# Two of a step's four stores begun by ScalarE's queue instead of the sync engine's, in the node stage of a four-layer graph network

## The chip, the cores and the metric

The kernel runs on one core of one Trainium2 chip. A core has TensorE (PE in the profile), VectorE (DVE), ScalarE (ACT), GpSimd (POOL) and the sync engine (SP), each with an instruction stream of its own that runs in the order in which it was written, and 16 DMA engines that move data between HBM and the on-chip memory. The engines meet through semaphores. A DMA is begun ("issued") by an instruction on one of the streams; the data then moves beside whatever that stream does next. The metric is the time of one execution in microseconds on the device, as the median of several runs.

## The reference, cut to what matters

Four layers of a graph network update 100,000 nodes of 160 numbers (64 scalars and 32 vectors of three). There are 25,000 edges, sorted by their destination. Layers 0 to 2 all have this form:

```python
sc = concat(xs @ W_self0 * a / sqrt(64), einsum(xv, W_self1) * a / sqrt(32))   # every node
conv = ...                                       # sums over a node's incoming edges
x = layernorm(x + sc + alpha * conv)             # every node
```

Layer 3 normalizes each node, adds attention over the incoming edges, and ends with a feed-forward block:

```python
x = node_input + proj(attention over incoming edges)
s2, v2 = eq_layernorm(x)
fs, fv = linear(s2, v2)                          # times the node's attribute a
y = x + linear(silu(fs[:, :128]), fv * sigmoid(fs[:, 128:]))
x = layernorm(node_input + y)
```

A node without an incoming edge needs no edge term in any layer. So the kernel first takes every node through all four layers as if it had no edges (the node stage), and keeps the rows before layers 1, 2 and 3 as tables in HBM; later stages gather rows of these tables for the edges and write over the rows of destination nodes.

## The kernel before, in words

`program` runs its stages one after the other, with a barrier between them: weights, the node stage (`all_nodes`), the index of the edges, three edge layers, and four stages for the attention. The change is in `all_nodes` alone.

`all_nodes` works on 250 nodes at a time, 125 partitions by J = 2 rows. There are eight lanes (buffers for eight such groups), and 100,000 / 2,000 = 50 rounds, so 400 lane steps. What one lane step does, each as a small function of lane n and round i:

- SP: `load` (L574 to L582) begins three transfers: `nodes_s_t` (65 partitions by 250 numbers, from a transposed copy of x), `nodes_v_t` (97 partitions by 250) and `nodes_z` (125 partitions by 2 rows of 164 numbers, from `rows`). `store1`, `store2` and `store3` (all L588) write the 125 by 2 rows before layers 1, 2 and 3 to their tables; `store_out` (L592 to L595) writes 125 by 2 rows of 160 numbers from `nodes_res` to `out`. That is seven transfers per lane step.
- DVE: `sum0` (L663) waits for the three loads of its lane and sums the rows; `add0` to `add2` (L673) add a layer's product from PSUM to the row; `widen0` to `widen2` (L683, L685) finish the variance, after which the row may be stored; then parts of layer 3.
- ACT: `var0` to `var2` (L749) square the rows, `copy1` and `copy2` (L738, L739) bring the transposed rows back from PSUM, `scale`, `ffn_copy` and `activate` serve layer 3, and `finish` (L759) writes the result to `nodes_res`.
- PE: transposes and products (L795, L796, L812, L814, L312 to L338). POOL: the mean (L612), roots, and part of layer 3.

The order on every engine comes from one table, `order`: each function has a begin, in planned units, with a spacing of `part = 8.40` between lanes. `staggered` folds the begins of all lanes into one round of 8 x 8.40 and sorts them, and `run_rounds` gives each engine its own functions in that order, in a loop over rounds. A begin therefore sets only the place of a function among the others of its engine. On SP this gives in every lane step: `load` of one lane, then `store3`, `store_out`, `store2` and `store1` of lanes that were loaded earlier. A store waits for the engine that wrote its rows (`widen` on DVE, `finish` on ACT); `add` of the next round waits until the store from that buffer has landed (`stored`), and so does `finish` (`out_stored`). At the end of the stage SP waits for all stores.

Of the kernel before, what the change touches and what calls it, by code (L numbers as in the profile page):

```python
# [14 lines left out]
J = 2  # L15
# [23 lines left out]
def count_at(t, i, engine, step):  # L39

    names = t["names"][engine]
    return i * len(names) + names.index(step) + 1


def prime(eng, t, engine):

    for n in range(t["lanes"]):
        eng.sem_inc(t[engine][n], len(t["names"][engine]))


def gate(eng, t):


    eng.sem_inc(t["turn"], 1)


def staggered(order, part, lanes):

    steps = []
    for step, begin in order:
        for n in range(lanes):
            behind, at = divmod(begin + n * part, lanes * part)
            steps.append((at, int(behind), n, step))
    return [(step, n, behind) for at, behind, n, step in sorted(steps, key=lambda entry: entry[0])]


def run_rounds(eng, rounds, order, part, steps, lanes=LANES):  # L70

    mine = [(step, n, behind) for step, n, behind in staggered(order, part, lanes) if step in steps]
    for step, n, behind in mine:
        if not behind:
            steps[step](n, 0)
    with eng.Fori(1, rounds) as i:
        for step, n, behind in mine:
            steps[step](n, i - behind)  # L80
    for step, n, behind in mine:
        if behind:
            steps[step](n, rounds - 1)
# [412 lines left out]
def all_nodes(nc, sem, sb, banks, inp, w, ffn, tables, out, nodes):  # L496
# [3 lines left out]
    lanes = NODE_LANES  # L500
    rounds = nodes // NODE_ROWS
    T = lanes * J
    x_loaded = [sem(f"nodes_x_loaded_lane{n}") for n in range(lanes)]
    stored = {l: [sem(f"nodes_table{l}_stored_lane{n}") for n in range(lanes)] for l in (1, 2, 3)}
    out_stored = [sem(f"nodes_out_stored_lane{n}") for n in range(lanes)]
    ready = sem("nodes_constants_ready")

    part = 8.40
    order = [("load", 0.0), ("sum0", 10.65), ("mean0", 11.22), ("mult0", 13.01), ("add0", 14.19), ("var0", 15.04),
# [4 lines left out]
             ("double", 39.85), ("measure", 40.25), ("merge", 41.02), ("square", 41.63), ("widen", 41.96),  # L514
             ("roots", 42.28), ("root_attr", 43.53), ("scale", 43.8), ("normalize", 44.7), ("ffn_turn", 46.14),
             ("ffn_copy", 48.01), ("hidden", 50.4), ("activate", 52.9), ("gates", 55.33), ("ffn_out", 56.65),
             ("residual", 58.87), ("out_measure", 59.72), ("out_merge", 60.47), ("out_widen", 66.09),
             ("out_roots", 66.34), ("offset_out", 67.99), ("finish", 70.39), ("store_out", 71.47)]

    done = {"pe": {"ffn_turn": "ffn_turned", "hidden": "ffn_hidden", "ffn_out": "ffn_out"},  # L520
            "act": {"scale": "ffn_scaled", "ffn_copy": "ffn_copied", "activate": "ffn_activated",
# [8 lines left out]
    for l in range(3):  # L530
# [3 lines left out]
    t = lane_steps(sem, "nodes", lanes,  # L534
                   **{e: [done[e][step] for step, begin in order if step in done[e]] for e in done})
# [6 lines left out]
    z = sb("nodes_z", [P, 4, T, ROW])  # L542
# [6 lines left out]
    root3 = sb("nodes_root3", [P, T])  # L549
    factor3 = sb("nodes_factor3", [P, T])  # L550
    offset3 = sb("nodes_offset3", [P, T])
# [4 lines left out]
    res = sb("nodes_res", [P, T, F])  # L556
    out_view = out.rearrange("(p r) f -> p r f", p=P)
    table_view = [x.rearrange("(p r) f -> p r f", p=P) for x in tables]
    x_t = inp["x_t"]

    def tiles(n):
        return slice(J * n, J * n + J)

    with nc.Block() as block:
        @block.sync
        def _(sp):
            for n in range(lanes):
                for l in (1, 2, 3):
                    sp.sem_inc(stored[l][n], 16)
                sp.sem_inc(out_stored[n], 16)  # L570
            sp.wait_ge(ready, 2)

            def load_x(n, i):

                sp.wait_ge(t["dve"][n], count_at(t, i, "dve", "added0"))
                gate(sp, t)
                rows = bass.ds(i * T + J * n, J)
                sp.dma_start(s0_t[0:VS, n, :].rearrange("f (j p) -> f j p", j=J), x_t[0:VS, rows, :]
                             ).then_inc(x_loaded[n], 16)
                sp.dma_start(v0_t[0:V + 1, n, :].rearrange("f (j p) -> f j p", j=J), x_t[MEAN:X, rows, :]  # L580
                             ).then_inc(x_loaded[n], 16)
                sp.dma_start(z[:, 0, tiles(n), :], table_view[0][:, rows, :]).then_inc(x_loaded[n], 16)  # L582

            def store_table(l):
                def store(n, i):
                    sp.wait_ge(t["dve"][n], count_at(t, i + 1, "dve", f"widened{l - 1}"))
                    gate(sp, t)
                    sp.dma_start(table_view[l][:, bass.ds(i * T + J * n, J), :], z[:, l, tiles(n), :]  # L588
                                 ).then_inc(stored[l][n], 16)
                return store  # L590

            def store_out(n, i):  # L592
                sp.wait_ge(t["act"][n], count_at(t, i + 1, "act", "out_normed"))
                gate(sp, t)
                sp.dma_start(out_view[:, bass.ds(i * T + J * n, J), :], res[:, tiles(n), :]  # L595
                             ).then_inc(out_stored[n], 16)

            run_rounds(sp, rounds, order, part, dict(load=load_x, store_out=store_out, store1=store_table(1),
                                                     store2=store_table(2), store3=store_table(3)), lanes)
            for n in range(lanes):  # L600
                for l in (1, 2, 3):
                    sp.wait_ge(stored[l][n], 16 * rounds + 16)
                sp.wait_ge(out_stored[n], 16 * rounds + 16)
# [126 lines left out]
        @block.scalar  # L730
        def _(act):
            prime(act, t, "act")
            act.wait_ge(ready, 2)

            def copy(l):
                def copy_turned(n, i):
                    act.wait_ge(t["pe"][n], count_at(t, i + 1, "pe", f"turned{l}"))
                    act.activation(s_t[0:VS, n, :], banks[n % 2][0:S + 1, 0:W], ACT.Copy)  # L738
                    act.activation(v_t[0:V + 1, n, :], banks[n % 2][0:V + 1, W:2 * W], ACT.Copy  # L739
                                   ).then_inc(t["act"][n], 1)  # L740
                return copy_turned

            def square_rows(l):

                def step(n, i):
                    act.wait_ge(t["dve"][n], count_at(t, i + 1, "dve", f"added{l}"))
                    for j in range(J):
                        k = J * n + j
                        ins = act.activation(x3[:, k, :], z[:, l + 1, k, 0:X], ACT.Square,  # L749
                                             bias=z[:, l + 1, k, MEAN:MEAN + 1], scale=-1.0,  # L750
                                             accum_out=total[:, l, k:k + 1])
                    ins.then_inc(t["act"][n], 1)
                return step

            def finish(n, i):
                act.wait_ge(t["dve"][n], count_at(t, i + 1, "dve", "out_offset"))
                act.wait_ge(out_stored[n], 16 * i + 16)
                for j in range(J):
                    ins = act.activation(res[:, J * n + j, :], ffn["y"][:, n, j, :], ACT.Identity,  # L759
                                         bias=out_offset[:, n, j:j + 1], scale=ffn["y_root"][:, n, j:j + 1])  # L760
                ins.then_inc(t["act"][n], 1)

            def scale(n, i):
                ffn_scale(act, ffn, t, i + 1, n, [x3[:, J * n + j, VS:X] for j in range(J)],
                          z[:, 3, tiles(n), A:A + 1].rearrange("p j o -> p (j o)"))

            run_rounds(act, rounds, order, part, dict(
                copy1=copy(1), copy2=copy(2), var0=square_rows(0), var1=square_rows(1), var2=square_rows(2),
                scale=scale, finish=finish,
                ffn_copy=lambda n, i: ffn_copy_turned(act, ffn, t, i + 1, n),  # L770
                activate=lambda n, i: ffn_activate(act, ffn, t, i + 1, n)), lanes)
# [1866 lines left out]
```

## Time and profile before

| | us |
|---|---|
| Median of three runs (11,328.65 to 11,331.06) | 11,330.98 |
| Profiled execution, its own time | 11,326.82 |
| Span of that execution, first to last instruction | 11,325.1 |
| Node stage within the span, about 47 to 4,674 | 4,627 |
| All later stages, 4,674 to the end | 6,651 |

Over the whole span PE is busy for 80%, DVE for 72%, POOL for 47% and ACT for 40% of the time. The node stage makes up about two fifths of the span and is steady: windows of 1,000 us from 500 us to 4,500 us differ by less than 2% in every engine's busy time. In the tables below, the idle time of an engine is given with what ended it ("<-"), and a DMA issue on SP is shown as `SPq ... DMA_DIRECT2D`; the duration of an issue is the time that the issuing instruction took, not the time in which the data moved.

### The profile page before, as it was taken

How to read it: one execution, taken by the hardware profiler on the slowest of the kernel's cores; microseconds unless marked ns; L12 is line 12 of the kernel's file. 1: busy time of each engine (PE TensorE's matmuls, PEld its weight loads, DVE VectorE, ACT ScalarE, POOL GpSimd, SP SyncE). 2: the span in 40 equal slices, each digit the busy share in tenths (PEclk: the TensorE clock that was granted, in tenths of full speed). 3: DMA queues.
4: the chain of work that ended last, by engine and by line, in shares of the span. 5: the costliest groups of instructions: out<-in, count | busy, mean ns of one | idle time of the engine just before them, and what ended most of it. 6: DMA issues, size and time to landing. Idle time of an engine off the chain costs nothing. (4 is left out here: it accounts for less than half of the span.)

```text
span 11325.1 us, 241587 instructions
## 1 busy us (share of the span) xinstructions
PE 9089.1 (80%) x58771; PEld 8291.2 (73%) x58771; DVE 8098.2 (72%) x40535; ACT 4475.4 (40%) x17107; POOL 5279.8 (47%) x6680
## 2 busy tenths in 40 slices
PE   7877787777778787799978887888588888849998
PEld 6777777777777777688866676777577777738888
DVE  5666666666666666688878887888688888877777
ACT  4555555555555555333322232333222222212222
POOL 3444444444444444577755554555444444423444
PEclk8888888888888888899999998999888888869999
DMA  2222222222222222233322222222111111111111
GB/s 68 85 86 85 85 86 85 86 86 85 86 86 85 86 85 85 70 77 77 77 63 68 68 67 59 57 57 57 39 40 40 39 39 40 39 32 51 53 54 48
DMA packets 988491, 753.89 MB, mean 67 GB/s; under 512 B 430970, under 2 KB 948478, under 8 KB 988048
## 3 DMA queue, kind: packets, MB, share of 16 engines
q1 hardware_dynamic: 823696, 587.78, 18.4%
q0 software_dynamic: 164352, 162.20, 6.0%
q14 instruction: 409, 3.35, 0.1%
q8 instruction: 34, 0.56, 0.0%
HBM read 362.41 MB, written 392.80 MB: 67 GB/s over the span
## 5 line engine op out<-in xcount | busy, mean ns | idle before, releaser
L749 ACT ACTIVATE nodes_x<-nodes_z 125x161 f32<-125x161 f32 x2400 | 1005.5, 422 | 1439.1 <-DVE nodes_z L673 1437.4
L127 PE MATMUL bank<-ident 128*128 128x128 f32 x10000 | 1478.0, 297 | 97.1 <-PEq L883 58.7
L127 PEld LDWEIGHTS bank<-ident 128*128 128x128 f32 x10000 | 1415.1, 213 | 145.5 <-issue 59.2
L814 PE MATMUL bank<-self_v,nodes_v_t 128*125 128x98 f32 x4800 | 1153.2, 328 | 0.0
L812 PE MATMUL bank<-self_s,nodes_s_t 128*125 128x65 f32 x4800 | 977.2, 291 | 150.9 <-DVE ffn_y L233 143.6
L812 PEld LDWEIGHTS bank<-self_s,nodes_s_t 128*125 128x125 f32 x4800 | 879.8, 223 | 226.6 <-issue 206.4
L612 POOL TENSOR_SCALAR nodes_z<-nodes_sum 125x2 f32<-125x2 f32 x400 | 113.2, 283 | 1987.4 <-DVE nodes_sum L663 1987.4
L673 DVE SCALAR_TENSOR_TENSOR nodes_z<-bank,nodes_z 125x162 f32<-125x162 f32 x2400 | 811.2, 380 | 273.7 <-PE bank L814 271.4
L1203 POOL DMA_INDIRECT table<-edge_new,edge_into_now x600 | 733.5, 1222 | 565.5 <-issue 516.4
L312 PE MATMUL bank<-ident,ffn_sn 125*65 125x125 f32 x800 | 264.6, 346 | 788.3 <-DVE ffn_sn L214 784.3
L663 DVE TENSOR_REDUCE nodes_sum<-nodes_z 125x2 f32<-125x322 f32 x400 | 195.4, 489 | 948.8 <-DMA nodes_z<-rows 948.8
L814 PEld LDWEIGHTS bank<-self_v,nodes_v_t 128*125 128x125 f32 x4800 | 865.6, 226 | 0.0
L1171 POOL DMA_INDIRECT edge_rows<-table,edge_ends_now x416 | 519.6, 1249 | 598.0 <-DVE edge_carry L1056 532.2
L312 PEld LDWEIGHTS bank<-ident,ffn_sn 125*65 125x65 f32 x800 | 134.9, 169 | 839.1 <-issue 836.3
L1437 ACT ACTIVATE edge_sums<-bank 125x163 f32<-125x163 f32 x600 | 151.3, 304 | 1282.8 <-PE bank L1525 1282.8
L1171 POOL DMA_INDIRECT edge_rows<-rows,edge_ends_now x416 | 505.0, 1214 | 220.7 <-DVE edge_carry L1056 123.5
L1768 POOL DMA_INDIRECT att_edge_rows<-table,att_edge_ends_now x416 | 511.0, 1228 | 194.0 <-POOL att_edge_ends_now L1761 97.9
L233 DVE SCALAR_TENSOR_TENSOR ffn_y<-bank,nodes_z,nodes_u 125x160 f32<-125x160 f32 x800 | 270.3, 379 | 414.0 <-issue 220.1
L1288 DVE SCALAR_TENSOR_TENSOR edge_msg<-bank,edge_y,edge_msg 125x65 f32<-125x65 f32 x1800 | 510.0, 283 | 32.0
L795 PE MATMUL bank<-ident,nodes_z 125*65 125x125 f32 x1600 | 510.3, 334 | 1.4 <-DVE nodes_z L673 1.3
L796 PE MATMUL bank<-ident,nodes_z 125*97 125x125 f32 x1600 | 503.7, 331 | 0.0
L338 PE MATMUL bank<-f_v,ffn_hid_v 128*125 128x160 f32 x1600 | 478.3, 390 | 0.0
(496 smaller groups left out, 30563.3 us busy)
## 6 DMA issues: line engine op xcount, KB each, us to landing
table<-nodes_z SPq DMA_DIRECT2D x1200, 160.2 KB
nodes_z<-rows SPq DMA_DIRECT2D x400, 160.2 KB
out<-nodes_res SPq DMA_DIRECT2D x400, 156.2 KB
nodes_v_t<-x_t SPq DMA_DIRECT2D x400, 94.7 KB
edge_dst_row<-dst SPq DMA_DIRECT2D x300, 122.1 KB
ordered<-edge_new SPq DMA_DIRECT2D x200, 160.2 KB
edge_rows<-ordered SPq DMA_DIRECT2D x200, 160.2 KB
dest_rows<-kept SPq DMA_DIRECT2D x100, 316.4 KB
```

The costliest lines, as they stand in the source:

```text
L127: pe.matmul(banks[2 * ((n + lead) % LANES) + odd][:, 0:128], w["ident"][:, :], w["ident"][:, :], start=True, stop=True)
L338: ins = pe.matmul(b[0:P, o:o + F], f["hid_v2"][:, n, c], f["w"]["f2_v2"][:, :], start=False, stop=True, skip_group_check=True)
L673: ins = v.scalar_tensor_tensor(z[:, l + 1, k, 0:A + 1], banks[2 + n % 2][0:P, o:o + A + 1], z[:, l, k, A:A + 1], z[:, l, k, 0:A + 1], ALU. ...
L749: ins = act.activation(x3[:, k, :], z[:, l + 1, k, 0:X], ACT.Square, bias=z[:, l + 1, k, MEAN:MEAN + 1], scale=-1.0, accum_out=total[:, l, ...
L795: pe.transpose(banks[n % 2][0:S + 1, j * P:(j + 1) * P], z[:, l, k, 0:VS], ident)
L796: ins = pe.transpose(banks[n % 2][0:V + 1, W + j * P:W + (j + 1) * P], z[:, l, k, MEAN:X], ident)
L812: pe.matmul(banks[2 + n % 2][0:P, o:o + VS], xs[:, n, c], w[f"self_s{l}"][:, :], start=True, stop=True)
L814: ins = pe.matmul(banks[2 + n % 2][0:P, o + MEAN:o + A + 1], xv[:, n, c], w[f"self_v{l}"][:, :], start=False, stop=True, skip_group_check= ...
L1171: p.indirect_dma_start(e["rows"][:, n, side, j, :], None, source, bass.IndirectOffsetOnAxis(ap=e["ends_now"][:, side, k:k + 1], axis=0)).t ...
L1203: p.indirect_dma_start(target, bass.IndirectOffsetOnAxis(ap=e["into_now"][:, k:k + 1], axis=0), e["new"][:, n, j, :], None, bounds_check=n ...
L1288: v.scalar_tensor_tensor(scalars, bank[0:P, o:o + 1 + S], y, scalars, ALU.mult, ALU.add)
L1768: p.indirect_dma_start(e["rows"][:, n, side, j, :], None, table, bass.IndirectOffsetOnAxis(ap=e["ends_now"][:, side, k:k + 1], axis=0)).th ...
```

## The change

`store3` and `store_out` are taken out of SP's functions and written again, with the same waits, transfers and semaphores, as functions of ACT. Their begins in the table are moved so that both follow `finish` (70.39, which folds to 3.19 of 8.40) on ACT: `store3` from 35.98 to 37.98 (folds to 4.38), `store_out` from 71.47 to 71.77 (folds to 4.57). The next function of ACT is `var1` (folds to 5.05).

```diff
-             ("store3", 35.98), ("root3", 36.68), ("offset3", 37.63), ("divide", 37.9), ("shift", 39.2),
+             ("store3", 37.98), ("root3", 36.68), ("offset3", 37.63), ("divide", 37.9), ("shift", 39.2),
...
-             ("out_roots", 66.34), ("offset_out", 67.99), ("finish", 70.39), ("store_out", 71.47)]
+             ("out_roots", 66.34), ("offset_out", 67.99), ("finish", 70.39), ("store_out", 71.77)]
...
-            def store_out(n, i):
-                sp.wait_ge(t["act"][n], count_at(t, i + 1, "act", "out_normed"))
-                gate(sp, t)
-                sp.dma_start(out_view[:, bass.ds(i * T + J * n, J), :], res[:, tiles(n), :]
-                             ).then_inc(out_stored[n], 16)
-
-            run_rounds(sp, rounds, order, part, dict(load=load_x, store_out=store_out, store1=store_table(1),
-                                                     store2=store_table(2), store3=store_table(3)), lanes)
+            run_rounds(sp, rounds, order, part, dict(load=load_x, store1=store_table(1), store2=store_table(2)), lanes)
...
+            def store3(n, i):
+                act.wait_ge(t["dve"][n], count_at(t, i + 1, "dve", "widened2"))
+                gate(act, t)
+                act.dma_start(table_view[3][:, bass.ds(i * T + J * n, J), :], z[:, 3, tiles(n), :]
+                              ).then_inc(stored[3][n], 16)
+
+            def store_out(n, i):
+                act.wait_ge(t["act"][n], count_at(t, i + 1, "act", "out_normed"))
+                gate(act, t)
+                act.dma_start(out_view[:, bass.ds(i * T + J * n, J), :], res[:, tiles(n), :]
+                              ).then_inc(out_stored[n], 16)
+
             run_rounds(act, rounds, order, part, dict(
+                store3=store3, store_out=store_out,
```

SP inside the loop, the lane step that loads lane 1, before. `table<-nodes_z` waiting for DVE's lane 5 is `store3`, the ones for lanes 7 and 0 are `store2` and `store1`; an `ISA` row is a register or semaphore instruction.

```order
L582 DMA nodes_z<-rows 125x328
L588 ISA [waits nodes_dve_steps_lane5]
L588 DMA table<-nodes_z 125x328
L595 ISA [waits nodes_act_steps_lane1]
L595 DMA out<-nodes_res 125x320
L588 DMA table<-nodes_z 125x328 [waits nodes_dve_steps_lane7]
L586 ISA
L588 DMA table<-nodes_z 125x328 [waits nodes_dve_steps_lane0]
L578 ISA [waits nodes_dve_steps_lane2]
```

The same place on SP now:

```order
L582 DMA nodes_z<-rows 125x328
L588 DMA table<-nodes_z 125x328 [waits nodes_dve_steps_lane7]
L586 ISA
L588 DMA table<-nodes_z 125x328 [waits nodes_dve_steps_lane0]
L578 ISA [waits nodes_dve_steps_lane2]
```

Two of the four stores between one load and the next are gone from SP; nothing else on it moved.

ACT inside the loop, the end of the lane step that finishes lane 1, before (L759 is `finish`, L749 `var1`):

```order
L302 ACTIVATE ffn_tanh<-bank 128x250
L759 ACTIVATE nodes_res<-ffn_y,nodes_out_offset,ffn_y_root 125x160 [waits nodes_out_stored_lane1,nodes_dve_steps_lane1]
L759 ACTIVATE nodes_res<-ffn_y,nodes_out_offset,ffn_y_root 125x160
L749 ACTIVATE nodes_x,nodes_square_total<-nodes_z 125x161 [waits nodes_dve_steps_lane7]
L749 ACTIVATE nodes_x,nodes_square_total<-nodes_z 125x161
```

The same place on ACT now, where L752 is `finish`, L763 `store3`, L769 `store_out` and L742 `var1`:

```order
L302 ACTIVATE ffn_tanh<-bank 128x250
L752 ACTIVATE nodes_res<-ffn_y,nodes_out_offset,ffn_y_root 125x160 [waits nodes_out_stored_lane1,nodes_dve_steps_lane1]
L752 ACTIVATE nodes_res<-ffn_y,nodes_out_offset,ffn_y_root 125x160
L763 ISA [waits nodes_dve_steps_lane5]
L763 DMA table<-nodes_z 125x328
L769 ISA [waits nodes_act_steps_lane1]
L769 DMA out<-nodes_res 125x320
L742 ACTIVATE nodes_x,nodes_square_total<-nodes_z 125x161 [waits nodes_dve_steps_lane7]
```

Both stores stand between `finish` and `var1`. `store_out` waits for the `finish` that ACT itself has just run.

## Rows read from the trace of the kernel before

**Rows 1.** Windows: stretch, length, busy us of PE, PEld, DVE, ACT, POOL; clock; DMA share; GB/s.

```profile
1500.00:2500.00 1000.00, 796.41 (x4872) 755.53 (x4873) 609.95 (x3140) 553.83 (x2175) 423.43 (x783) 0.82 0.27 86
...
4600.00:4700.00 100.00, 55.04 (x328) 49.16 (x327) 54.61 (x275) 36.87 (x138) 33.45 (x58) 0.74 0.18 56
```

**Rows 2.** Waits of the engines, 500 to 4,500 us: us in total, times, longest.

```profile
ACT nodes_x L749 <- DVE nodes_z L673: 1254.8, 571, 5.1
DVE nodes_sum L663 <- DMA nodes_z<-rows: 828.7, 308, 4.5
...
PE bank L312 <- DVE ffn_sn L214: 698.7, 303, 4.1
```

**Rows 3.** Waits of the sync engine's queue, the same stretch.

```profile
SPq L54 <- DVE nodes_z L683: 3.7, 11, 0.6
SPq L54 <- DVE nodes_z L685: 3.0, 9, 0.8
```

**Rows 4.** SP's issue instructions, same stretch: count, shortest/median/longest ns, first and last start.

```profile
L578 SPq DMA_DIRECT2D nodes_s_t<-x_t x349: 334/827/1352, 500.9 to 4498.6; - x175
...
L580 SPq DMA_DIRECT2D nodes_v_t<-x_t x348: 251/267/397, 502.4 to 4488.3; - x174
...
L582 SPq DMA_DIRECT2D nodes_z<-rows x348: 4463/4905/4944, 502.9 to 4488.8; - x174
...
L588 SPq DMA_DIRECT2D table<-nodes_z x1045: 262/936/1511, 500.2 to 4497.6; - x175
...
L595 SPq DMA_DIRECT2D out<-nodes_res x348: 648/786/1242, 509.2 to 4495.6; - x174
```

**Rows 5.** SP's first issues of the stage, timeline: start, duration, instruction.

```profile
47.97 0.25 SPq L580 DMA_DIRECT2D nodes_v_t<-x_t  x1
48.27 0.64 SPq L582 DMA_DIRECT2D nodes_z<-rows  x1
...
49.68 4.76 SPq L582 DMA_DIRECT2D nodes_z<-rows  x1
67.90 0.28 SPq L588 DMA_DIRECT2D table<-nodes_z  x1
```

**Rows 6.** DMA, 47 to 67 us in 40 slices: share in tenths, GB/s; packets.

```profile
DMA  0005045331000000343300000000000000000000
GB/s 0 0 0 124 20 57 102 123 127 59 22 24 24 22 23 24 62 86 116 114 32 22 22 22 22 22 24 24 18 0 0 0 0 0 0 0 0 0 0 0
DMA packets 613, 0.67 MB, mean 33 GB/s; under 512 B 38, under 2 KB 612, under 8 KB 612
```

**Rows 7.** DMA, 2,000 to 2,023 us (two lane steps) in 40 slices.

```profile
DMA  0012233333335433310000223333333335333100
GB/s 21 23 30 44 72 112 125 118 104 118 119 116 147 132 100 116 112 54 31 25 23 23 43 64 118 113 84 102 72 92 123 119 112 163 114 116 117 61 25 23
```

**Rows 8.** Transfers by line, 500 to 4,500 us: count and KB (of 1,024 bytes) of each.

```profile
table<-nodes_z SPq DMA_DIRECT2D x1045, 160.2 KB
...
out<-nodes_res SPq DMA_DIRECT2D x348, 156.2 KB
nodes_v_t<-x_t SPq DMA_DIRECT2D x348, 94.7 KB
nodes_s_t<-x_t SPq DMA_DIRECT2D x349, 63.5 KB
```

**Rows 9.** ACT's timeline: `finish`, and the next step's `var1` with the idle time before it.

```profile
2005.13 0.92 ACT L759 ACTIVATE nodes_res<-ffn_y,nodes_out_offset,ffn_y_root 125x160 f32<-125x160 f32 x2
2010.69 0.43 ACT L749 ACTIVATE nodes_x<-nodes_z 125x161 f32<-125x161 f32 x1 [4.63 <-DVE nodes_z L673]
...
2033.46 0.43 ACT L749 ACTIVATE nodes_x<-nodes_z 125x161 f32<-125x161 f32 x1 [2.28 <-DVE nodes_z L673]
```

## The prediction, made before the changed kernel ran

> **What bounds the kernel now.** I read the windows first, for the size of the stage that is changed. In the steady part of the node stage, PE is busy for 796 us of 1,000, DVE for 610, ACT for 554 and POOL for 423, and the DMA engines move 86 GB/s at a mean share of 0.27 [rows 1]: no engine is full. The length of a lane step comes from the starts of SP's first issue: (4498.6 - 500.9) / 348 = 11.488 us [rows 4], and 400 of them are 4,595 us, nearly the whole stage.
>
> The waits tell which way to look. DVE waits 828.7 us of the 4,000 for the loaded rows, and ACT (1,254.8 us) and PE (698.7 us) wait for DVE behind it [rows 2]. So the compute engines are fed by the loads. Who holds the loads? SP begins them, and SP waits for nobody: 6.7 us in all [rows 3]. Its seven issues fill the step: by medians 0.827 + 0.267 + 4.905 + 3 x 0.936 + 0.786 = 9.59 us, and the other 1.89 us lie between them, 0.27 us each [rows 4]. The easy reading is that SP's issuing is the bound, so that two issues fewer must shorten the step. The reader should not stop there: an issue can be long because the instruction is, or because something below it takes no more.
>
> The stage's first issues decide between the two. With nothing under way, `nodes_v_t` was issued in 0.25 us, the rows in 0.64 us and a table store in 0.28 us; the second load of rows already took 4.76 us [rows 5]. The instruction is short; what makes it long is what stands ahead of it. In that same stretch the DMA rates show what [rows 6]: SP had issued the last of two lanes' six loads at 49.68 + 4.76 = 54.44 us and issued nothing until 67.90 us [rows 5], but data moved from about 48.5 to 61.5 us, 13 us for 0.65 MB, and in the last 4 us at only 18 to 24 GB/s, while other slices reach 114 to 127. A transfer was crawling on its own with SP idle.
>
> The steady part repeats it. In two lane steps the rate is never under 21 GB/s; stretches of 21 to 31 GB/s, with a share that rounds to 0 tenths, alternate with stretches of about 100 to 125 GB/s at 3 tenths [rows 7]. The high level is 118 / 23 = 5.1 times the low one, and five of 16 engines are 3 tenths. I read that as one DMA engine that works all the time and four that share the work for part of it. The transfer that runs on the one engine alone must be a load that comes in every step; `nodes_v_t`, 94.7 KB or 97,000 bytes [rows 8], fits the slow tail after the first loads: 97,000 / 22.7 GB/s = 4.3 us. If the five row transfers are spread over five engines, the loaded one carries a fifth of (4 x 160.2 + 156.2) KB [rows 8], 163,000 bytes, and with `nodes_v_t` 260,000 bytes per step. At the rate that it shows when alone, 21 to 25 GB/s and 23 in the middle, that is 10.4 to 12.4 us, 11.3 in the middle, with `nodes_s_t` still to be added (nothing to a fifth of 65,000 bytes: 0 to 0.6 us). The step is 11.488 us. So one DMA engine is full, and SP's long issues are its queue seen from above.
>
> Which transfer lies on how many engines is inferred here. A page of the Trainium skill has a rule for it (DMA: Bandwidth & Descriptors, "Why a DMA increments its semaphore by 16 and not by 1"): a transfer uses the largest number of engines up to 16 that divides its first dimension, and every engine used ends with a small semaphore write. By it 125 partitions go to 5 engines, 97 to one and 65 to 13, which is 19 small writes for the three loads of a lane; the trace agrees, since the two lanes at the start left 38 packets under 512 bytes [rows 6].
>
> **The change part by part.** SP loses one of three table stores and the store of the result in each lane step. As SP's own time that is 0.936 + 0.786 + 2 x 0.27 = 2.26 us [rows 4]. But the bytes stay: the same transfers of 160.2 and 156.2 KB go to the same memory, and the loaded engine still has 260,000 bytes to move per step. Its 11.488 us remain, so SP's remaining five issues stretch, or SP begins to wait for `widen`, and neither costs anything while that engine has work queued. I take 0 us for this part. The other end, 2.26 us per step, is a rival below.
>
> On this the skill has a rule that speaks against the change (same page, "Issuing engines are not separate DMA queues"): transfers begun by different engines run on the same 16 DMA engines and interleave, and a second issuer saves only issue time. No run here has shown two issuers in this stage yet; by that rule the sum is the same 0 us.
>
> ACT gains two issues per step. The trace shows none of ACT's, so I bound them by SP's: 0.28 us into an idle system [rows 5], 4.94 us at the worst behind a slow load [rows 4]. The nearest rows are those of the same two stores on SP, 0.94 and 0.79 us at the median, and I take their sum, 1.7 us. They stand between `finish` and `var1`, where ACT was idle for 4.63 us in one step and 2.28 in another [rows 9], and 1,254.8 / 348 = 3.6 us in the mean [rows 2]. That wait hides them: `var1` waits for a sum of DVE, which waits for the load. Behind them on ACT are `var1`, `ffn_copy`, `var0` and `copy2`; DVE's `widen` and PE's next product wait for those, and SP's stores for `widen`. Were the cover gone, every us over it would cost up to 400 us. The waits of the two stores themselves are met when ACT comes to them: `widen2` folds to 2.11 of 8.40 on DVE, ahead of 4.38, and `finish` has just run. I take 0 us.
>
> The ends of the stage: in its last 100 us the engines are half idle and DMA moves 56 GB/s [rows 1], so the last stores may come out a few us sooner or later; I take 0, and keep 5 us either way. The later stages do not change.
>
> Sum: 0 us on a profiled time of 11,326.8 us, which lies 4.2 us under the median of 11,331.0. Forecast 11,331 us.
>
> **The rivals.**
>
> *A second queue moves the loaded engine faster.* When one queue feeds it, it shows 22 to 24 GB/s alone; the high stretches, up to 123 GB/s over five engines, are 24.6 each [rows 6, 7]. If two queues kept it at 24.6 for all of `nodes_v_t`, that load would take 3.94 us in place of 4.27, and the stage 0.33 x 400 = 130 us less: 11,200. If all 260,000 bytes ran at it, 10.57 us against 11.3 gives 290 us: 11,040. For it: no row shows two queues. Against it: the steps fit one rate within its scatter. Chance 0.10, between 11,020 and 11,300.
>
> *The issues are the bound after all*, or ACT's stores go to other DMA engines than SP's. Then the step falls by 2.26 us to 9.23, and PE with 0.796 x 11.488 = 9.15 us of work per step [rows 1] is the next bound, about equal. 2.26 x 400 = 905 us: 10,425. For it: SP never waits, and DVE waits for the loads. Against it: the 0.25 to 0.64 us of the free issues, and data that crawl while SP is idle. Chance 0.11.
>
> *Slower: ACT is held in its issues.* ACT works 0.554 x 11.488 = 6.36 us per step [rows 1], which leaves 5.13. If `store3` is held behind a slow load as SP's rows are, 4.9 us, and `store_out` behind it as long as a table store can be, 1.5 us [rows 4], ACT needs 12.8 us per step and becomes the bound: 1.3 x 400 = 510 us, 11,840. It decides from the point where the two issues take over 5.1 us together, and costs up to 400 us per us above it; where they stay between 3.6 and 5.1, it costs little. For it: ACT's stores come right after `finish`, at a time when SP pushes its loads. Against it: if ACT is late, SP waits for `widen`, less is queued, and ACT is held less. Chance 0.17, half of it under 11,600.
>
> The skill has a mechanism for this last one (Perfetto Trace Analysis, "DMA Instruction — HWDGE (DVE, Sync)"): one descriptor generator is shared by the issuing engines and locked for the whole of an issue. No row of this trace can show it, since only SP issues in this stage.
>
> **How the numbers follow.** No measurable change, 11,331 us with its own range of 0.2% (11,308 to 11,354, about what a measurement of this kernel can tell from no change): 0.62. Faster through a faster engine 0.10, faster because issues are the bound 0.11: together 0.21. Slower 0.17. The range leaves out the 10,425 us (0.11) and the worse half of the slower case (0.085), 0.195 in all: from 11,020, the lower end of the faster engine, to 11,600.
>
> **What would show it.** Right: starts of `nodes_s_t` still 11.49 us apart, rates that never leave the floor of 21 GB/s, DVE still waiting for the load by about 2 us a step, ACT's issues under 2 us together with a shorter wait ahead of `var1`, and SP's five issues longer than before or followed by waits. Wrong: gaps at 0 GB/s in the steady part, or a floor above 25, or a step that is shorter by the 2.26 us (the issues were the bound), or ACT issues of several us with DVE no longer waiting for loads but for ACT.

## The result, and the profile after

The changed kernel takes 11,265.3 us (median of three runs, 11,258.1 to 11,266.9) against 11,331.0: 66 us or 0.58% less, ratio 0.9941 with a 95% interval of 0.9918 to 0.9964. I had forecast no change, with 0.21 on "faster". The time lies inside the range that I gave, but the gain is clear of the noise, so the forecast of no change was wrong.

The gain is in the node stage. The next stage's first issue comes at 4,606.06 us where it came at 4,674.24, 68.2 us sooner, and the span fell by 68.7 us (11,325.1 to 11,256.4). SP's issues in the steady part of the changed kernel (columns as in [rows 4]; L588 is now `store1` and `store2` alone), and ScalarE's two new ones:

```profile
L578 SPq DMA_DIRECT2D nodes_s_t<-x_t x354: 334/786/2097, 507.8 to 4499.7; - x177
...
L582 SPq DMA_DIRECT2D nodes_z<-rows x354: 1710/5890/7371, 500.1 to 4489.8; - x177
...
L588 SPq DMA_DIRECT2D table<-nodes_z x708: 285/440/1680, 505.6 to 4499.0; - x177
...
L763 ACTq DMA_DIRECT2D table<-nodes_z x354: 268/269/273, 501.1 to 4490.4; - x177
...
L769 ACTq DMA_DIRECT2D out<-nodes_res x354: 268/269/269, 502.7 to 4492.2; - x177
```

A lane step now takes (4499.7 - 507.8) / 353 = 11.309 us, where it took 11.488 [rows 4]: 0.18 us less, 72 us in 400 steps. ScalarE's issues take 0.27 us each, whatever SP's are doing; SP's issue of the rows became longer, 5.89 us for 4.91 at the median.

The waits of the engines and of SP's queue, 500 to 4,500 us, as in [rows 2, 3]:

```profile
ACT nodes_x L742 <- DVE nodes_z L666: 1211.2, 591, 5.0
DVE nodes_sum L656 <- DMA nodes_z<-rows: 752.5, 294, 4.4
```

```profile
SPq L54 <- DVE nodes_z L678: 679.1, 351, 6.9
SPq L54 <- DVE nodes_z L676: 184.3, 341, 1.1
```

DVE still waits for the load, 752.5 / 354 = 2.1 us per step, and ACT for DVE. SP, which waited 7 us in all before, now waits 863 us for DVE's `widen`: it has issues to spare, and they buy nothing, because the transfers that it has already begun are still queued. The DMA rates show that, in the stretch of [rows 7], with SP's queue (q1) and ScalarE's (q10):

```profile
DMA  3335431013332222333333353333210000012233
GB/s 91 98 104 123 142 116 44 25 43 89 94 105 79 96 87 103 125 101 85 99 115 103 117 178 115 109 107 97 105 70 27 23 23 25 23 38 62 66 123 94
...
q1 hardware_dynamic: 1153, 1.33, 18.7%
q10 hardware_dynamic: 525, 0.65, 8.8%
```

The floor of 23 to 27 GB/s is still there, and nothing falls under it. What differs in this window is the length of the slow stretches: one still has five slices in a row under 28 GB/s, the other is filled up to a single slice of 25 between 44 and 43.

### The profile page after: what moved, and what is told of

Its sections match the earlier page's. It is cut to its first block and busy times, and to the rows that moved or that the text cites. A ratio compares the mean times of both kernels' runs of the same rounds, so it can differ in the third digit from the quotient of the medians.

```text
span 11256.4 us, 241883 instructions
## 1 busy us (share of the span) xinstructions
PE 9065.6 (81%) x58771; PEld 8278.3 (74%) x58771; DVE 8111.4 (72%) x40535; ACT 4477.8 (40%) x17107; POOL 5288.4 (47%) x6680
## 5 line engine op out<-in xcount | busy, mean ns | idle before, releaser
L742 ACT ACTIVATE nodes_x<-nodes_z 125x161 f32<-125x161 f32 x2400 | 1005.7, 422 | 1379.9 <-DVE nodes_z L666 1377.7
L1774 POOL DMA_INDIRECT att_edge_rows<-table,att_edge_ends_now x416 | 511.9, 1231 | 194.0 <-POOL att_edge_ends_now L1767 97.9
L620 POOL TENSOR_SCALAR nodes_x<-nodes_z,nodes_factor,nodes_offset 125x161 f32<-125x161 f32 x800 | 377.3, 482 | 201.7 <-DVE nodes_offset L685 201.7
```

What stands on the lines that cost most here:

```text
L1774: p.indirect_dma_start(e["rows"][:, n, side, j, :], None, table, bass.IndirectOffsetOnAxis(ap=e["ends_now"][:, side, k:k + 1], axis=0)).th ...
```

## The experiments

Times are medians, each set against runs of the kernel before on the same chip (11,327.5, 11,325.2 and 11,328.0 us in the three sets that were timed). Where I speak of packets on the loaded engine, I count as the rule in the prediction has it: `nodes_v_t` puts all its 97 pieces and one semaphore write on that engine, each row transfer a fifth of 125 pieces and one, `nodes_s_t` a thirteenth of 65 and one, 98 + 5 x 26 + 6 = 234 per step.

**Is one DMA engine the bound?** The load of `nodes_v_t` cut into 96 partitions and one; the bytes and the issuing engine stay. `split_before` has this cut in the kernel before, `split_after` in the changed one.

```diff
-                sp.dma_start(v0_t[0:V + 1, n, :].rearrange("f (j p) -> f j p", j=J), x_t[MEAN:X, rows, :]
+                sp.dma_start(v0_t[0:V, n, :].rearrange("f (j p) -> f j p", j=J), x_t[MEAN:X - 1, rows, :]
                              ).then_inc(x_loaded[n], 16)
+                sp.dma_start(v0_t[V:V + 1, n, :].rearrange("f (j p) -> f j p", j=J), x_t[X - 1:X, rows, :]
+                             ).then_inc(x_loaded[n], 16)
...
-                    v.wait_ge(x_loaded[n], 48 * i + 48)
+                    v.wait_ge(x_loaded[n], 64 * i + 64)
```

> The kernel before with the load of nodes_v_t cut into 96 partitions and one, all on SP: eight issues per step in place of seven, same bytes. If one DMA engine is full because that load lies on it alone, its part of 97,000 bytes is spread, 98 of its 234 packets fall to about 10, and the engine needs 7.2 us per step; the compute engines set the step then, about 9.2 to 9.8 us by TensorE's 9.15 us of work: 10,400 to 10,650. If SP's issuing is the bound, one issue more gives no gain: 11,331 or over, up to 0.5 us per step more.

> The changed kernel with the same cut of the load. If the full engine was all that held both kernels, this runs as the cut kernel without the change, within 0.5%. If SP's issue time becomes the next bound once the engine is free, this one is faster than the cut kernel without the change by up to 2 us per step.

The cut kernel takes 10,124.2 us, ratio 0.8938 (0.8923 to 0.8953): 1,201 us less, with one issue more on SP. Its views follow: SP's first issue (500 to 4,000 us) and its issue of the rows (500 to 3,000 us), what DVE still waits for the load (500 to 4,000 us), a window from 500 to 3,000 us (columns as in [rows 1]), and the rates from 2,000 to 2,020 us:

```profile
L578 SPq DMA_DIRECT2D nodes_s_t<-x_t x345: 334/335/842, 505.3 to 3430.4; - x173
...
L584 SPq DMA_DIRECT2D nodes_z<-rows x293: 262/263/397, 507.2 to 2993.8; - x147
```

```profile
DVE nodes_sum L665 <- DMA nodes_z<-rows: 66.4, 88, 1.1
```

```profile
500.00:3000.00 2500.00, 2277.38 (x16448) 2165.30 (x16447) 2027.39 (x10576) 1861.32 (x7343) 1438.50 (x2646) 0.93 0.36 116
```

```profile
GB/s 115 111 121 118 118 115 110 128 96 109 120 182 202 172 111 115 88 116 112 123 113 118 112 112 122 120 123 153 194 218 92 104 109 123 69 45 47 42 37 20
```

The step is (3430.4 - 505.3) / 344 = 8.503 us, the slow stretches are gone but for a few slices, DVE hardly waits for loads any more (66 us in 3,500), SP's issue of the rows takes 0.26 us in place of 4.91, and PE is the busiest engine with 91%. So the reading of the profile stands: the long issues of SP were the queue of one DMA engine, and its bytes, not SP's time, made the step. With the engine free the change is worth less than nothing: `split_after` takes 10,159.9 us (0.8969, 0.8954 to 0.8984), 36 us more than `split_before` in the same set (10,155 to 10,170 us against 10,119 to 10,142). That is 0.35%, inside the 0.5% that I had expected; what costs the 36 us is open.

That leaves the question why the changed kernel gained at all, when the bytes on the loaded engine are the same. I had two theories at first. *Packets*: two queues with work keep the engine fuller, so the gain goes with the bytes in the second queue. *Ends*: the end of each transfer holds up its queue for a moment, which the other queue fills, so the gain goes with the number of transfers. Four kernels move one thing each:

`v_load_act` begins the load of `nodes_v_t` alone on ScalarE's queue; `s_load_act` does the same with `nodes_s_t`.

```diff
-    order = [("load", 0.0),
+    order = [("load", 0.0), ("load_part", 0.01),
...
+            def load_part(n, i):
+                act.wait_ge(t["dve"][n], count_at(t, i, "dve", "added0"))
+                gate(act, t)
+                act.dma_start(v0_t[0:V + 1, n, :].rearrange("f (j p) -> f j p", j=J), x_t[MEAN:X, bass.ds(i * T + J * n, J), :]
+                              ).then_inc(x_loaded[n], 16)
...
-                sp.dma_start(v0_t[0:V + 1, n, :].rearrange("f (j p) -> f j p", j=J), x_t[MEAN:X, rows, :]
-                             ).then_inc(x_loaded[n], 16)
```

> The kernel before, with only the smallest load (nodes_s_t, 65 partitions) begun by ScalarE's queue; all stores stay on SP. Known so far: moving two stores took the lane step from 11.488 to 11.309 us (0.18 us, 0.09 per store). Theory packets (the loaded DMA engine moves packets faster while two queues hold work for it, so the gain goes with the bytes in the second queue): this transfer has only a sixth or less of a store's bytes on that engine, gain 0.02 us per step, 8 us, about 11,323. Theory ends (each transfer's end holds up its own queue for a moment and the other queue fills that moment, so the gain goes with the number of transfers in the second queue): 0.09 us per step, 36 us, about 11,295.

> The kernel before, with only the slow load (nodes_v_t, 97 partitions, by my reading all on one DMA engine) begun by ScalarE's queue. Theory packets: it has about 98 of that engine's 234 packets per step against 52 in the changed kernel, gain 0.18 x 98 / 52 = 0.34 us per step, 135 us, about 11,195. Theory ends: one transfer, 0.09 us, 36 us, about 11,295. If the engines were not shared by the queues, the step would fall by whole microseconds.

`stores4_act` is the changed kernel with the other two stores on ScalarE's queue as well, behind `finish` like the first two. Against the changed kernel:

```diff
-             ("turn1", 16.17), ("widen0", 16.29), ("store1", 16.6), ("copy1", 16.94), ("mult1", 19.82),
-             ("add1", 21.0), ("var1", 21.85), ("turn2", 22.3), ("widen1", 23.3), ("store2", 23.57),
+             ("turn1", 16.17), ("widen0", 16.29), ("store1", 21.18), ("copy1", 16.94), ("mult1", 19.82),
+             ("add1", 21.0), ("var1", 21.85), ("turn2", 22.3), ("widen1", 23.3), ("store2", 29.59),
...
-            run_rounds(sp, rounds, order, part, dict(load=load_x, store1=store_table(1), store2=store_table(2)), lanes)
+            run_rounds(sp, rounds, order, part, dict(load=load_x), lanes)
...
-                store3=store3, store_out=store_out,
+                store1=store_table(1), store2=store_table(2), store3=store_table(3),
+                store_out=store_out,
```

> The changed kernel with the other two stores on ScalarE's queue too, so that SP only loads. Both theories of the gain: twice that of the changed kernel, 0.36 us per step, 143 us, about 11,190. If the gain came only from SP getting ahead with its loads, it should be used up by two stores: about 11,265, as the changed kernel. A risk: ScalarE waits for the widened rows, which costs if they come late.

`store3_act` is the changed kernel with the store of the result back on SP and at its old begin:

```diff
-                store3=store3, store_out=store_out,
+                store3=store3,
...
-            run_rounds(sp, rounds, order, part, dict(load=load_x, store1=store_table(1), store2=store_table(2)), lanes)
+            run_rounds(sp, rounds, order, part, dict(load=load_x, store_out=store_out, store1=store_table(1),
+                                                     store2=store_table(2)), lanes)
```

> Half of the change: the store of the third table on ScalarE's queue, the store of the result still on SP. Both theories (packets, ends): half the gain, 0.09 us per step, 33 us, about 11,298. If the gain hangs on one of the two stores alone, about 11,331 or 11,265.

| On ScalarE's queue | packets | us | ratio (95%) | step, us | gain per step |
|---|---|---|---|---|---|
| `nodes_s_t` | 6 | 11,324.2 | 0.9996 (0.9987 to 1.0005) | 11.482 | 0.006 |
| third table | 26 | 11,315.6 | 0.9990 (0.9981 to 0.9999) | 11.454 | 0.034 |
| third table, result (the change) | 52 | 11,265.3 | 0.9941 (0.9918 to 0.9964) | 11.309 | 0.180 |
| `nodes_v_t` | 98 | 11,138.9 | 0.9833 (0.9820 to 0.9846) | 11.008 | 0.480 |
| all four stores | 104 | 11,116.1 | 0.9812 (0.9799 to 0.9826) | 10.975 | 0.513 |

The steps are worked out from first and last start as above. *Ends* falls: one transfer gains 0.006, 0.034 or 0.48 us. *Packets* gets the order right but no size: half the change gains a fifth of it, and the gain per packet runs from 1 to 5 ns. That SP merely gets ahead falls too, since the last two stores brought more again.

**Bare transfers.** The disputed cost by itself: a stretch ahead of the node stage in which nothing but transfers of this kernel's shapes run. It is one function, put before `all_nodes`:

```diff
+    L, T = [(load, k) for k in range(16)], [(store, k) for k in range(32)]
+    mixed = [step for k in range(8) for step in (L[k], *T[4 * k:4 * k + 4])]
+    phases = [(L, []), (L[:8], L[8:]), (T, []), (T[:16], T[16:]), (mixed, []), (L[:8], T), (mixed[:20], mixed[20:]),
+              ([(small, k) for k in range(64)], [])]
```

> The kernel before with a stretch of bare transfers put ahead of the node stage, each group begun when the last has landed: (1) 16 loads of the nodes_v_t shape on SP's queue; (2) the same, 8 on SP's and 8 on ScalarE's; (3) 32 stores of the table shape on SP's; (4) the same, 16 and 16; (5) 8 loads and 32 stores in turn (one load, four stores) on SP's; (6) the 8 loads on SP's, the 32 stores on ScalarE's; (7) half of the turns of (5) on each queue; (8) 64 transfers of one number on SP's. Theory packets in flight (one queue alone does not keep the loaded engine full; a second one adds work in flight, whatever its direction): (2) under (1), (4) under (3), (6) and (7) under (5), each by about 5% (the moved load gained 0.48 us of its step with 196 of the 234 packets then in two queues, 2.4 ns of 49 each). Theory directions (the engine gains only where a load and a store run side by side): (2) as (1), (4) as (3), (6) under (5) by 5%. Sizes: (1) about 70 us, (3) about 42, (5) about 77. (8): 64 x 2 packets; the end of a transfer costs the engine more than a packet only if this takes much over 64 x 0.1 us beyond the issue time.

> The bare transfers again, to see their scatter: groups (1) to (6) of the first probe, run twice in a row. The first probe gave 70.5 us for loads on one queue, 69.3 on two; 50.0 for stores on one, 50.5 on two; 82.9 for loads and stores in turn on one queue and 78.4 with the loads on one and the stores on the other. Theory directions: the last gap, 4 to 5 us, comes back both times, the first two stay within 1.5 us of zero. Theory packets in flight: the gaps are scatter, and all three pairs average to one relative gain.

The first issue of each group in the first probe, from the timeline of SP (start, duration of the issues in a row, their number; a row merges issues of a line that follow each other, also across groups):

```profile
31.21 121.58 SPq L849 DMA_DIRECT2D probe_got<-x_t  x24
171.04 84.52 SPq L853 DMA_DIRECT2D probe_rows_out<-probe_rows  x48
271.53 0.23 SPq L849 DMA_DIRECT2D probe_got<-x_t  x1
...
354.43 78.64 SPq L849 DMA_DIRECT2D probe_got<-x_t  x9
...
513.68 19.12 SPq L856 DMA_DIRECT2D probe_tiny<-rows  x64
```

Groups 2, 4 and 7 show on ACT, where no earlier group's issues hide their start:

```profile
101.71 53.18 ACTq L849 DMA_DIRECT2D probe_got<-x_t  x8
220.99 202.63 ACTq L853 DMA_DIRECT2D probe_rows_out<-probe_rows  x48
432.85 0.24 ACTq L849 DMA_DIRECT2D probe_got<-x_t  x1
```

A group begins when the one before it has landed, so the differences of the starts are the times of the groups:

| Group | one queue | two queues | change |
|---|---|---|---|
| 16 loads | 70.50 | 69.33 | -1.7% |
| 32 stores | 49.95 | 50.54 | +1.2% |
| 8 loads, 32 stores | 82.90 (in turn) | 78.42 (loads on SP, stores on ACT) | -5.4% |
| the same, half of each on either queue | | 80.83 | -2.5% |
| 64 transfers of one number | 19.12 to issue | | |

The second probe gave 70.47 and 69.39, 49.95 and 50.48, 83.05 and 78.35 us (the last from 354.35 us to the first issue behind it, at 432.70), and in its second pass 70.49, 69.43, 49.92, 50.88, 83.04 and about 78.4. The scatter is under 0.5 us. The 32 stores had been expected to take 42 us and the mix 77; they took 50 and 83. A second queue that moves the same way gains or loses a little; loads in one queue beside stores in the other gain 4.5 to 4.7 us in 83, 5.4 to 5.7%. Taking turns within one queue gains at most 2.3 us: 8 loads alone are half of 70.5 and 32 stores 49.95, together 85.2 us, and these hold half a start more than the mix. The 64 small transfers took 0.30 us each, their issue time, so the end of a transfer holds up nothing that shows here. So *directions* replaces both theories: the loaded engine gains where a load and a store run on it side by side. In this mix that is 4.5 us for the 784 packets of the eight loads, 5.7 ns for each pair.

**A load beside a load.** `z_load_act` moves the load of the rows alone, with the code of the two loads above.

> The kernel before with only the load of the rows (nodes_z) on ScalarE's queue, so that it runs beside nodes_v_t, load beside load. By packets (26 on the loaded engine, as a store has) theory packets in flight gives the gain of a single moved store or more, 0.03 to 0.13 us per step, 12 to 50 us, about 11,295; theory directions gives none, 11,327. It also tells whether the rows come in earlier for VectorE, which by the reading that one engine is full changes nothing.

11,302.2 us, ratio 0.9978 (0.9969 to 0.9988), a step of (3993.4 - 500.2) / 306 = 11.416 us: 0.07 us gained where *directions* had none. The waits show what became of the load (500 to 4,000 us):

```profile
DVE nodes_sum L662 <- DMA nodes_v_t<-x_t: 660.5, 233, 5.5
```

The rows, now in a queue of their own, land first, and DVE waits for `nodes_v_t`. What they met can be counted. The trace has the start, the duration, the bytes and the queue of every packet, and the pieces differ: 1,000 bytes for the transposed loads, 1,312 for the rows, 1,280 for the result. The engine of a packet is not given, but the load of `nodes_v_t` can be followed on its one engine, since each of its packets begins where the last one ends. In the kernel before there is 44.1 ns from one to the next (339 steps). The load's 97 packets and five of `nodes_s_t` so take 4.50 us of the step of 11.488, and the 125 row packets, with the semaphore writes, share the other 6.99 us: 55.9 ns each. A load's packet and a row's, one after the other, take 100.0 ns. In `z_load_act` 17 of the load's packets per step have one of the rows' load behind them, and the two take 97.9 ns. So most of the rows did meet the load, and 17 x 2.1 ns is 0.04 us; the rest of the 0.07 is open. A load beside a load gains a little (as among the bare transfers, 1.7%), not nothing, and in this *directions* missed.

**The place of the store.** If what the store meets decides, its time matters. The gain of the half change at two places on ACT: before the first squares of the step, `var1` (`store3_act`, above), and after them.

`both_late` is the changed kernel with these two lines; `store3_late` is `store3_act` with the first of them alone.

```diff
-             ("store3", 37.98), ("root3", 36.68), ("offset3", 37.63), ("divide", 37.9), ("shift", 39.2),
+             ("store3", 39.1), ("root3", 36.68), ("offset3", 37.63), ("divide", 37.9), ("shift", 39.2),
...
-             ("out_roots", 66.34), ("offset_out", 67.99), ("finish", 70.39), ("store_out", 71.77)]
+             ("out_roots", 66.34), ("offset_out", 67.99), ("finish", 70.39), ("store_out", 72.8)]
```

> The half change (store of the third table on ScalarE's queue) with that store placed after the first squares of the step in place of before them, some 5 us later, when by the rates of the kernel before the loaded engine is still at the slow load and not at the stores. Theory directions: the store now meets a load on the engine, gain up to 26 x 5.7 ns = 0.15 us per step, I expect 0.08 to 0.15 (30 to 60 us, about 11,285), against 0.034 us at the early place. Theory packets in flight: the place does not matter, 0.034 us, about 11,315.

> The changed kernel with both stores placed after the first squares in place of before them. Theory directions: 0.2 to 0.3 us per step against 0.18 at the early place, 80 to 120 us, about 11,225. Theory packets in flight: as the changed kernel, about 11,262.

`store3_late` takes 11,228.1 us, ratio 0.9912 (0.9898 to 0.9925), 100 us less than before, where the early place gained 12: the same single transfer on the same queue, moved behind one function of ACT. Its step is (4390.8 - 503.8) / 346 = 11.234 us, 0.254 less. `both_late` takes 11,227.3 (0.9910, 0.9896 to 0.9923).

I had chosen the late place by the floor in the rates, which I took for the slow load. That reading is wrong in the steady part. Two stretches of the kernel before at the floor, the tail of the first loads (57.5 to 59.5 us) and the steady part (2,022 to 2,023.5 us):

```profile
DMA packets 44, 0.04 MB, mean 22 GB/s; under 512 B 0, under 2 KB 44, under 8 KB 44
...
DMA packets 27, 0.03 MB, mean 23 GB/s; under 512 B 1, under 2 KB 27, under 8 KB 27
```

22 GB/s for 2 us is 1,000 bytes per packet, the load; 23 GB/s for 1.5 us is 1,330 for each of the 26 packets that are not a semaphore write, which are rows. Of the packets in all half microseconds under 30 GB/s from 500 to 4,400 us, 98% are rows: there the loaded engine works off rows while the four others have nothing to move. The load runs while those are busy, at 99 GB/s in the mean. Nor does the rate at an issue tell what the store meets: its first packet comes 1.9 us (early place) or 3.0 us (late place) behind the issue, at the median.

The packets tell it. Per step, the load's packets that have one of the other queue behind them, the time of such a pair, and what the pairs are worth against 100.0 ns:

| Kernel | pairs per step | ns for a pair | pairs x saving, us | gain per step, us |
|---|---|---|---|---|
| `store3_act` (early) | 4 | 97.3 | 0.01 | 0.034 |
| `z_load_act` | 17 | 97.9 | 0.04 | 0.072 |
| `both_late` | 15 | 95.9 | 0.06 | 0.257 |
| `store3_late` | 21 | 95.8 | 0.09 | 0.254 |
| the change | 29 | 95.2 | 0.14 | 0.180 |
| `stores4_act` | 64 | 95.2 | 0.31 | 0.513 |
| `v_load_act` | 92 | 94.8 | 0.48 | 0.480 |

The late store meets the load, 21 times out of 25, and the early one hardly does: that much was expected. A pair with a store saves 4 to 5 ns (2.7 in the few pairs of the early place), one with the rows' load, whose packets have the same size, 2.1. With each transfer's own time the gap is wider: in the 251 steps of the kernel before that can be followed from load to load, a packet of the rows' load takes 54.7 ns and one of the third table's store 56.5, so that the first pair saves 0.9 ns and the late store's 4.8. So the direction counts, and not the size alone. The pairs give all of the gain of `v_load_act` and three quarters of that of the change.

The size is not settled for the late places. One store has 26 packets on the loaded engine, and at 5.7 ns a pair the late place should gain 0.15 us at most; it gained 0.25, of which the pairs give 0.09. The load's other packets are no faster there (44.1 ns), so the rest lies in the rows' own packets, most of which have nothing of the second queue beside them. Why these became faster, and why the second late store adds nothing, stays open; the number of pairs alone does not order the gains.

## Why the prediction was wrong

- **The bound was read rightly.** One DMA engine is full, SP's issue times are its queue, and the five issues that stay stretch or turn into waits for `widen`: the rows of 5.89 us and the 863 us of waits are what I said would show it. The cut load proves it with 8.50 us per step.
- **The step that failed** is "Its 11.488 us remain" in the change part by part. It took the loaded engine's pace as a property of its bytes. The pace depends on what lies next to each other on the engine: 83.0 or 78.4 us for the same bare transfers, and in the changed kernel 95.2 ns for a load's packet and a store's of the other queue where one after the other they take 100.0, 29 times per step. The step fell to 11.309 us; 0.14 of the 0.18 us are these pairs, the rest is open. No row of the trace before could show this case, since only one queue was in use.
- **The floor was misread, without harm to the sum.** `nodes_v_t` runs on one engine, as I said, and is the slow tail after the first loads; but the floor of the steady part is rows (26 packets of about 1,330 bytes in 1.5 us). What I call a slow load there, in the rivals and in what I expected of `store3_late`, is that engine's rest of rows. The 260,000 bytes and the 23 GB/s stay as they are.
- **The rival that came about** is the second queue that moves the loaded engine faster, with 0.10. Its price was 130 us with the slow load as the thing sped up, 0.33 us per step; measured were 0.18 us and 66 us. It gave the second queue a higher rate whatever that queue carries. That was not right: two queues of loads gained 1.7%, two queues of stores lost 1.2%.
- **The rule on the side of "no change"** (the Trainium skill, DMA: Bandwidth & Descriptors, "Issuing engines are not separate DMA queues") says that a second issuer saves only issue time. That the two queues share the DMA engines agrees: packets of both take turns on the loaded one, 95.2 ns for two. That nothing but issue time can be saved does not: 5.4 to 5.7% of a mix of loads and stores were. For the forecast of no change 0.62 was too much, since nothing in the trace bore on the second half of the rule.
- **ACT's issues** were taken as 1.7 us for both and cost 0.54; the slower rival, held issues, has no trace at all: 268 to 273 ns in 708 issues, while SP's were held up to 7.37 us. The page that I named for it (the Trainium skill, Perfetto Trace Analysis, "DMA Instruction — HWDGE (DVE, Sync)") has one generator, locked for the whole of an issue; these rows show no such hold. Where ScalarE's own queue is full its issues are held too: 8 loads took 53.18 us to issue in the first probe.
- **SP's issues as the bound** is refuted: SP now waits 2.4 us per step, and an issue more on SP went with 1,201 us less. Nor do ScalarE's stores go to other engines: their packets run between the load's.
- **The cut kernel** came out 276 us under the lower end of what I expected. I had taken TensorE's 9.15 us of work per step as fixed. It is 0.911 x 8.503 = 7.75 us there, at a granted clock of 0.93 in place of 0.82.

## What to carry to other kernels

Before an issue queue that is never idle is taken for the bound, look at what one issue takes when nothing is queued, and whether the DMA rate has a floor at the pace of one engine; the cure is then to spread the transfer that lies on one engine (97 partitions cut into 96 and one: 10.6%), not to move issues. Moving a transfer to a second queue pays a little where it puts a store beside a load on a full engine, and its place on the second engine's stream decides how much: 12 or 100 us for the same store. A low rate does not say which transfer is slow: divide the bytes by the packets. Once no engine is full, the move can cost, here 36 us.

## What was not expected of the hardware

- Loads and stores side by side on one DMA engine take 5.4 to 5.7% less time than in turn on one queue (78.4 against 83.0 us), while two queues in one direction change the time by -1.7% (loads) and +1.2% (stores).
- In the changed kernel an issue of ScalarE's takes 0.27 us while SP's issue of the rows takes 5.9 us at the median, and in the probe ScalarE's are held as well once its own queue is full, so the hold belongs to a queue, not to all issues.
- In the cut kernel TensorE is granted 0.93 of its clock (a mean over its two levels, 1.2 and 2.4 GHz) with 91% of the time busy, against 0.82 with 80% before [rows 1], when it stood up to 4.1 us at a time waiting for DVE behind the load [rows 2]. So TensorE took 9.15 us for the work of a step while it was kept waiting and 7.75 us once it hardly was.
